# Attention and quantised feed-forward, batches in a pipeline: the unmasked program placed behind the branch, and four moves in the first two batches

## The reference

```
def weight_quant(w):
    scale = 1.0 / clip(mean(abs(w)), 1e-05)
    return clip(round(w * scale), -1, 1) / scale
...
x = x + attention(layernorm(x), ctx, causal_mask, padding_mask)
h = gelu(silu(bitlinear158(layernorm(x), w1, b1)))          # 512 -> 2048
x = x + bitlinear158(layer_norm(h, ln_g, ln_b), w2, b2)     # 2048 -> 512
```

## Time and profile before

| | us |
|---|---|
| median of 3 runs | 610.38 |
| lowest and highest | 608.64 to 612.68 |
| the profiled execution | 610.75 |
| its span, first to last instruction | 608.7 |
| PE busy | 519.6 (85%) |
| DVE busy | 494.3 (81%) |
| ACT busy | 352.0 (58%) |
| POOL busy | 137.1 (23%) |

### The profile page before, as it was taken

How to read it: one execution, slowest core, us unless ns; L and a number is a source line. 1 busy time by engine, 2 the same in 40 slices (tenths; PEclk the granted TensorE clock), 3 DMA queues, 4 the chain that set the end, 5 groups by cost and what they waited for, 6 DMA issues and landing times.

```text
span 608.7 us, 8894 instructions
## 1 busy us (share of the span) xinstructions
PE 519.6 (85%) x3352; PEld 286.4 (47%) x3374; DVE 494.3 (81%) x728; ACT 352.0 (58%) x424; POOL 137.1 (23%) x105
## 2 busy tenths in 40 slices
PE   4958498599989999999999999999959988797556
PEld 4845324364457355645564556455514532343322
DVE  4657966987699978997899888988896899738895
ACT  1224183517684957586748673877277648578621
POOL 5103021300621061106110611221130103303030
PEclk9975889599989999999999999999969996989878
DMA  5789357926523650365036611671127111200001
GB/s 192 263 243 347 122 166 201 374 82 202 120 60 113 172 117 31 118 198 113 35 112 197 137 34 42 203 163 39 41 61 161 44 41 36 54 0 0 36 35 36
DMA packets 32994, 72.17 MB, mean 119 GB/s; under 512 B 7167, under 2 KB 14529, under 8 KB 29950
## 3 DMA queue, kind: packets, MB, share of 16 engines
q1 hardware_dynamic: 31222, 67.06, 37.8%
q0 software_dynamic: 576, 4.19, 1.7%
q10 hardware_dynamic: 1152, 0.31, 0.3%
HBM read 46.50 MB, written 20.61 MB: 110 GB/s over the span
## 4 chain that ended last, share of the span: by engine, by line
PE 60%; DVE 11%; issue 10%; ACT 8%; DMA 6%; POOL 3%; SPq 1%; ACTq 0%; DVEq 0%; POOLq 0%
PE FF L864 8%; PE FF L682 7%; PE PV L804 7%; PE S L771 6%; PE PV L787 6%; PE FF L913 6%; ACT PT L1085 5%; PE S L745 5%; PE PV L745 2%; PE FF L866 2%; DVE negm L1359 2%; PE FF L878 2%; DMA num<-o_raw 2%; PE FF L703 1%; PE FF L713 1%
## 5 line engine op out<-in xcount | busy, mean ns | idle before, releaser
L1085 ACT ACTIVATE PT<-S 128x1024 f32<-128x1024 f32 x128 | 123.6, 1031 | 29.1 <-PE S L771 28.7
L1359 DVE TENSOR_REDUCE negm<-S 128x4 f32<-128x1024 f32 x88 | 105.7, 1215 | 29.0 <-PE S L745 27.4
L771 PE MATMUL S<-Q,K 100*128 100x512 bf16 x256 | 77.6, 410 | 23.9 <-ACT PT L1085 16.1
L787 PE MATMUL PV<-PT,vaug 128*32 128x256 f32 x1024 | 72.4, 403 | 0.6 <-ACT PT L1085 0.6
L864 PE MATMUL FF<-w1t,xqT 128*128 128x512 bf16 x242 | 64.0, 384 | 9.5 <-ACT work L1116 4.3
L745 PE MATMUL S<-K,Q 97*128 97x256 bf16 x352 | 55.9, 286 | 10.5 <-issue 6.4
L804 PE MATMUL PV<-wo_sb,num 128*128 128x512 f32 x128 | 60.5, 618 | 4.5 <-POOL num L489 4.5
L1116 ACT ACTIVATE work<-FF,s 128x512 f32<-128x512 f32 x56 | 38.4, 687 | 40.3 <-PE FF L866 40.2
L1359 DVE TENSOR_REDUCE negm<-PV 128x4 f32<-128x1024 f32 x40 | 48.8, 1219 | 7.1 <-PE PV L745 6.7
L771 PEld LDWEIGHTS S<-Q,K 100*128 100x128 bf16 x256 | 18.3, 100 | 73.8 <-ACT PT L1085 53.7
L682 PE MATMUL FF<-xnT,wq_sb 128*128 128x256 f32 x224 | 52.0, 389 | 0.2 <-ACT xnT L1052 0.2
(11 more groups left out here) (197 smaller groups left out, 860.5 us busy)
## 6 DMA issues: line engine op xcount, KB each, us to landing
Q<-q_d SPq DMA_DIRECT2D x15, 768.0 KB
q_d<-part SPq DMA_DIRECT2D x8, 768.0 KB, 3.6
x_sb<-in_x SPq DMA_DIRECT2D x8, 512.0 KB, 3.7
ctx_sb<-in_ctxT SPq DMA_DIRECT2D x8, 512.0 KB, 4.2
work<-in_w SPq DMA_DIRECT2D x4, 1024.0 KB, 14.8
q_d<-part SPq DMA_DIRECT2D x8, 512.0 KB, 3.1
xb_sb<-in_x SPq DMA_DIRECT2D x8, 512.0 KB, 4.0
work<-in_w POOLq DMA_DIRECT2D x4, 1024.0 KB, 8.1
```

Of the source, the lines that this page charges most:

```text
L771: last = pe.matmul(where, K[0:ROWS_2, g, kt * P:(kt + 1) * P], Q[0:ROWS_2, g, 2 * pair:2 * pair + 2, :], start=not masked, stop=True)
L787: last = pe.matmul(PV[32 * r:32 * r + 32, g % 4, :], vaug[:, c % 2, kt, g, :], PT[:, n % PT_SLOTS, r, :], start=(kt == 0), stop=(kt == TT ...
L1085: act.activation(PT[:, n % PT_SLOTS, :, :], ST[n % 2][:], ACT.Exp, scale=0.25).then_inc(S["pt_made"], 1)
L1359: dve.tensor_reduce(negm[:, t, R * g:R * g + R], RING_1[n % 3][:], AX.X, ALU.max, negate=True).then_inc(S["max_made"], 1)
```

## The change

1. `flag_i` now holds 1 where the mask's rows agree, and the unmasked program stands directly behind the branch; the masked one is the else part, and a jump over it closes the unmasked program.
2. x of batch 2 is turned behind all 16 first scores of batch 0 instead of behind the eighth, and Q of batch 2 is projected behind the turning of batch 0's maxima instead of between the scores. DVE norms x of batch 2 behind the eighth maximum instead of the second. ACT sums all four chunks of w1 before it copies the turned x of batch 2.
3. On SP, wo, the output bias and the bias rows of the first layer move behind the maxima of batch 0, and x of batch 3 too.
4. w2 comes in two pairs of chunks: the first when DVE has read w1 out of `work` (`w_step` at 2), the second when the rows of batch 1 have landed, as all four did.
5. DVE does the first two passes over w1 ahead of the rests of Q of batch 2.

```diff
@@ SP, body (start-up and later bodies)
                     query_parts(1)
                     key_parts(1)
-                    weights_and_biases()
                     return
                 w = next_front(a)
-                if w is not None and w + 1 < B:
+                if w is not None and w + 1 < B and c > 0:
                     load_x(w + 1)
                 if c is not None:
                     maxima(c)
+                if at_start(c):
+                    load_x(w + 1)
+                    weights_and_biases()
                 if w is not None:
                     query_parts(w)
@@ POOL
-            def second_weights():
-                pool.wait_ge(S["w1_done"], 1)
-                pool.wait_ge(S["rows_in1"], 16 * ROW_LOADS * 2)
-                for n in range(4):
+            def second_weights(half):
+                if half == 0:
+                    pool.wait_ge(S["w_step"], 2)
+                else:
+                    pool.wait_ge(S["rows_in1"], 16 * ROW_LOADS * 2)
+                for n in range(2 * half, 2 * half + 2):
                     cols = slice(2048 * n, 2048 * n + 2048)
                     pool.dma_start(work[:, cols], w2[:, cols]).then_inc(S[f"w2_chunk{n}"], 16)
...
+                if at_start(c):
+                    second_weights(0)
                 if w is not None and w + 1 < B:
                     norm_1(w + 1)
                     norm_1_apply(w + 1)
                 if at_start(c):
-                    second_weights()
+                    second_weights(1)
@@ PE
                     weight_sum(c)
+                if at_start(c):
+                    project_q(2)
                 if w is not None:
                     project_q(w)
...
-            def first_body(general):
-
-                with pe.If(general):
+            def first_body(plain):
+
+                with pe.If(plain):
+                    batches(False)
+                with pe.Else():
                     batches(True)
-                with pe.Else():
-                    batches(False)
 
             def batches(masked):
                 pe.wait_ge(S["c_identb"], 1)
                 for n in range(16):
                     scores_1(0, n, masked)
-                    if n == 7:
-                        turn_x(2)
-                    if n in (8, 10, 12, 14):
-                        project_q(2, [(n - 8) // 2])
+                turn_x(2)
@@ ACT, start-up
-                    weight_abs_sum(0, range(1))
+                    weight_abs_sum(0)
                     turned_x(2)
-                    weight_abs_sum(0, range(1, 4))
@@ DVE
-                dve.tensor_copy(flag_i[:], flag_f[:, 0:1]).then_inc(S["k_flagi"], 1)
+                dve.tensor_copy(flag_i[:], flag_f[:, 1:2]).then_inc(S["k_flagi"], 1)
...
                     for n in range(16):
                         maximum(0, n)
-                        if n == 1:
+                        if n == 7:
                             norm_1(2)
...
+                if at_start(c):
+                    quantise_weight(0, w1t[:].rearrange("p k n -> p (k n)"))
                 if w is not None:
                     query_rests(w)
...
                 if at_start(c):
-                    quantise_weight(0, w1t[:].rearrange("p k n -> p (k n)"))
                     quantise_weight_end(0, w1t[:].rearrange("p k n -> p (k n)"), "w1_done")
```

## The result

| | before | changed |
|---|---|---|
| median, us | 611.44 | 606.07 |
| lowest and highest | 608.64 to 613.28 | 602.87 to 607.29 |
| runs | 10 | 10 |
| the profiled execution | 610.75 | 606.96 |
| its span | 608.7 | 605.0 |

The ratio is 0.9911 with a 95% interval of 0.9887 to 0.9935: 5.4 us faster, where 15.4 were forecast (595 us, range 592 to 603.5). The sign was right, the size and the range wrong.

The account below looks back on a forecast made before the run. Bound by PE work (60% of the chain of waits), winnable only in the start-up, 136 of 609 us. Terms -6.3, -5.1, +3.8, -2.0, -4.5, -1.5, closing jump 0, sum to -15.6: 610.75 to 595.1, forecast 595, range 592 to 603.5.

Parts of the forecast that it names:

- Part 1: Branch before batch 0's first scores: falling through instead of jumping lets scores start at 35.3 instead of 41.59; -6.3 us.
- Rival A: At the branch: fall-through as dear as the jump, the stall belonging to the compare; +6.1, 601.2 us; chance 0.12.
- E: At PE's end: the closing jump over the masked program is not covered; +4.3, 599.4 us; chance 0.04.
- Parts 2 and 3 of the sum: Batch 0: turning at 58.0, Q of batch 2 behind it, second scores at 67.5 lasting 18.3; -5.1, +3.8, -2.0 us.
- Rival C: PE's clock stays at 1.2 GHz through Q of batch 2 and the second scores; +7.1, 602.2 us; chance 0.08.
- landing at 81. Slack 5 us: Rows of batch 1: 7.3 MB from 61 take 20 us, landing at 81, 5 us before first scores want them.
- rival D: SP's queue floods at 200 GB/s or less; batch 1's rows land at 97 to 100; 614 us; chance 0.05.
- 5.17 us into the first scores: Batch 1: w2's second pair goes at 91.0, ends 96.4; reciprocals' product is through at 103.5 to 105.1.
- rival B: Batch 0's reciprocals stay slow, delayed by the w2 pair in flight; +4.5 +1.5, 601.1 us; chance 0.12.
- -4.5 (wait): Before batch 0's output projection: PE's 4.47 us wait for POOL's product of the reciprocals goes.
- Everything won before that point moves the end by as much: From batch 2's K projection (136.31 before, 120.7 forecast) the old order holds, so the whole start-up gain reaches the end.

Follow-up runs that it names:

- branch_undone: Changed kernel with the masked program directly behind the branch again and the unmasked one reached by the jump; 611.06 us, ratio 0.9983.
- branch_only: Kernel before with only the branch changed, so the unmasked program stands directly behind it; 608.61 us, ratio 0.9953.
- q_strewn: Changed kernel with x and Q of batch 2 strewn among batch 0's first scores again, norm and sums as before; 612.70 us, ratio 1.0013.
- w2_together: Changed kernel with all four chunks of w2 at their old place behind the rows of batch 1; 604.97 us, ratio 0.9892.
- w2_behind_rows: Changed kernel with w2's first pair issued only when the first half of batch 1's rows has landed; 604.47 us, ratio 0.9886.
- rests_first: Changed kernel with the rests of Q of batch 2 ahead of the two passes over w1 again; 604.58 us, ratio 0.9906.
- loads_behind_rows: Changed kernel with context of batch 2 and residual of batch 0 issued behind the first half of batch 1's rows; 604.43 us, ratio 0.9884.
- combo_pair_early: combo_both with w2's second pair issued behind the first half of batch 1's rows instead of both halves; 604.84 us, ratio 0.9887.
- w2_around_rec: Changed kernel with wo, biases, x of batch 3 early; w2's first pair behind half of batch 1's rows, second behind the reciprocals' reads; 611.26 us, ratio 0.9992.
- branch_and_q: Kernel before with only the branch change and the moved x and Q of batch 2; 604.93 us, ratio 0.99.
- combo_both: Changed kernel with wo and output bias early, only bias rows behind the maxima, context and residual behind both halves of batch 1's rows; 603.09 us, ratio 0.9861.
- combo_half: As combo_both, but context and residual stand behind the first half of batch 1's rows only; 603.30 us, ratio 0.9863.
- combo_rests: combo_both with the rests of Q of batch 2 ahead of the two passes over w1 again; 605.09 us, ratio 0.9901.

## Why the prediction was wrong, step by step

**Part 1, nearly right.** The branch took 88 ns, under 1 us as asked, and the first score started at 35.02 (35.3 forecast). Rival A is out, and so is E: the closing jump took 3343 ns and ended 3.4 us before SP. By the rule of the Trainium skill (Runtime: NRT & Kernel Launch, Instruction fetch mechanics) it had to stall; its 3343 ns agree, and they were hidden. Its worth at the turning is 4.7 us (branch_undone 62.59, changed 57.92); for branch_only it is 6.0 against the first profile of before and 3.8 against the second.

**Parts 2 and 3 of the sum, right.** Turning 57.92 (58.0), Q of batch 2 from 58.56 in 8.65 us (58.4, 9.1), second scores at 67.05 (67.5), the last values through at 85.7 (85.8). Rival C is out. q_strewn shows part 2 at 6.6 us in the median, with the rest of the change in place.

**The step that failed: "landing at 81. Slack 5 us".** It divided 7.3 MB by 364 GB/s, for 20 us from 61; measured were 31.4. The rows came at 92.4, 6.6 us later than the 85.8 at which PE wanted them. Of 61 to 92.5 us the profile has 8.64 MB, at a mean of 274 GB/s. The bytes alone (the second half of the rows is among them) would still have fitted the slack: 8.64 at 364 are 23.7 us, to 84.7. The pace did not: gaps in the first 11 us, and 200 to 228 GB/s at full share at the end. That the things ahead of the rows set their landing is shown: w2_together, w2_behind_rows, rests_first and loads_behind_rows each take one of them away, and each removes 5 us or more of the hole. This is rival D's mechanism short of its size (it had 97 to 100, at a chance of 0.05).

**"5.17 us into the first scores", the reciprocals, too short by 0.6 to 2.2 us.** The trip took 10.6 us (100.32 to 110.93). The sum had 8.4 to 10.0 (3.7 for the write, 4.7 to 6.3 for the reads), rival B 13.8, so with half of w2 beside it about half of the delay is left; combo_pair_early shows 6.3 with w2 all but through. The write also left 7.9 us into the first scores instead of 6.9. So the term "-4.5 (wait)" came to -3.2 (PE waited 1.30), with PE slow itself. The profile names DVE, whose last maximum is

```profile
112.06 1.21 DVE L1363 TENSOR_REDUCE negm<-S 128x4 f32<-128x1024 f32 x1
```

but POOL's product (110.93 + 2.34) ends at 113.27 like that maximum, and PE needs both. From the first scores to the projection it took 20.95 us instead of 18.65, its start at 1.2 GHz, and the projection 5.08 instead of 4.3.

**The sum.** K of batch 2 came at 130.42, 9.7 us later than the 120.7 forecast: 6.6 (rows) + 2.3 (first scores to projection) + 0.8 (projection); DVE's chain behind it took 11.97, as forecast. With 2.2 from the next point it is all that is missing between the profiled 606.96 and the 595.1 of the sum.

**"Everything won before that point moves the end by as much", wrong by 1 to 3 us.** In the profile K of batch 2 came 5.9 us earlier and the end 3.7. Part 1 gives 1.1 of it back in one body, as shown. The rest lies in the last 175 us, is there in branch_undone too, and was not found.

**Even with the rows in time the forecast would have failed.** The versions whose first scores wait 0.2 us or less have medians of 603.1 to 605.1 (w2_around_rec 611.3), not 595, because the bytes are the same: in this stretch rows, w2, loads, denominators and reciprocals want the same engines, and whichever is put ahead, the next one is late. In all of them but branch_and_q these are the denominators, for which DVE waits 1.5 us (combo_both, combo_half) to 6.0 (combo_pair_early), a wait that the prediction put at nothing: it dates the trip from where DVE stood before and asks for no landing of the denominators. In branch_and_q and w2_together it is the reciprocals, in w2_around_rec w2 itself as well. No version sends the denominators ahead of loads and w2, so what that would give is open.

## What to carry over

When a change moves transfers into a stretch that is already full, count the landing time of what is needed next at the pace that its own kind shows (here 200 to 228 GB/s where rows out of DRAM were most of what moved), not at the best rate of the trace, and do it for the small transfers behind it too: 8 KB of denominators held DVE up to 6.0 us. Where the profile names an engine as the releaser, read what that engine was waiting for itself. A slack worked out that way is part of the forecast's range, not a condition. And undo each part separately: here two parts of five did all the work, each gave little or nothing without the other (part 1 alone 2.9 us; part 2 with parts 3 to 5 1.1; parts 1 and 2 together 6.4), and the other three moved a wait from one engine to another.

## What the runs showed of the hardware

- A compare-and-branch on PE's sequencer took 77 to 88 ns when the next instruction was its target (14 versions), against 7606, 7446 and 6346 ns in the three profiles where it jumped over the masked program. The Trainium skill (Advanced Engine Details and Errata, Control Flow Timing) gives about 108 ns; the fall-through agrees, the jumps don't.
- The jump over the same program cost 3343 ns at the end (3333 to 3874 in the 14 versions), where the transfer engines had little to do, and 6346 to 7606 ns in the start-up. Whether the traffic makes the difference no run tried.
- A DVE operation that takes 0.17 to 0.22 us elsewhere took 2.08 to 2.37 us when it started inside a POOL sum over 128x1024 of about 2.4 us, and ended within 0.1 us of the sum's end (changed kernel: 391.01 + 2.36 and 390.98 + 2.36; combo_both: 386.60 + 2.08 and 386.29 + 2.37). In branch_undone the POOL sum itself took 3.35 us, beside other DVE work.
- Two busy queues moved about equally many packets, not bytes: 238 of w2 (1.75 MB) and 268 of SP's queue (0.76 MB) from 91 to 97 us of combo_pair_early, 153 (1.04 MB) and 166 (0.85 MB) from 86 to 92 of combo_rests.
- The write and read-back of the reciprocals took 6.3 us with w2 all but through, 10.6 to 10.9 beside 2 MB of it and 13.8 beside 4 MB.
